# Queries and keys turned by the projection's products and placed by DMAs, in a transformer block written out by hand

## What is computed

```python
x = x + 0.5 * ffn(layernorm(x))      # silu(x @ gate.T) * (x @ up.T), 1024 hidden, @ down.T
x = x + attn(layernorm(x))
x = x + 0.5 * ffn(layernorm(x))
# attn: x_n = x / max(norm(x), 1e-12) * 256 ** 0.5 * gamma
# qkv = x_n @ w_qkv: 16 query heads, 4 key heads, 4 value heads, 64 wide
# q = q * cos + rotate_half(q) * sin; k likewise (cos, sin by row and feature)
# causal softmax(q k.T / 8) v for each head (key head j serves heads j, 4+j, 8+j, 12+j), then @ w_out
```

## Time and profile before

| | us |
|---|---|
| time, median of 3 runs (lowest to highest) | 605.05 (603.68 to 605.48) |
| the profiled execution: its time, and its span | 604.62, 602.8 |
| opening, six turns, ending | 100.0, 416.5, 86.3 |
| busy in the span: PE, DVE, ACT, POOL | 572.0, 494.9, 386.1, 361.9 |
| mean clock granted to PE (1 is 2.4 GHz) | 0.994 |

### The profile page before, as it was taken

One profiled execution on the slowest core, in us unless ns is written; L12 is line 12 of the kernel. 1 busy time (PEld: TensorE's weight loads), 2 busy tenths in 40 slices (PEclk: granted clock), 3 DMA queues, 4 the chain that ended last, 5 costly groups with the idle time before them and its releaser, 6 DMA issues.

```text
span 602.8 us, 13310 instructions
## 1 busy us (share of the span) xinstructions
PE 572.0 (95%) x4230; PEld 531.9 (88%) x4230; DVE 494.9 (82%) x1410; ACT 386.1 (64%) x1021; POOL 361.9 (60%) x322
## 2 busy tenths in 40 slices
PE   6889988999999999999999999999999999878997
PEld 4777777999989999899989999899998999767887
DVE  4879887989789987999879986999879897898642
ACT  4544992499626993489715994379824996279711
POOL 1747764577637673586746775486645766476423
PEclk8989999999999999999999999999999999999999
DMA  7500000000000000000000000000000000000000
GB/s 246 181 15 1 1 2 17 2 2 21 1 17 0 0 17 17 0 0 0 17 17 0 0 17 0 17 0 0 17 17 0 0 0 0 17 2 1 1 18 19
DMA packets 7208, 10.60 MB, mean 18 GB/s; under 512 B 656, under 2 KB 5136, under 8 KB 7184
## 3 DMA queue, kind: packets, MB, share of 16 engines
q1 hardware_dynamic: 7184, 10.29, 5.3%
HBM read 8.19 MB, written 2.10 MB: 17 GB/s over the span
## 4 chain that ended last, share of the span: by engine, by line
PE 66%; DVE 9%; ACT 9%; issue 8%; POOL 6%; DMA 2%; SPq 1%; POOLq 0%; DVEq 0%; ACTq 0%
PE bank L796 46%; PE bank L805 9%; PE bank L883 5%; ACT probs L429 4%; PE bank L861 3%; PE bank L857 2%; DVE xn L579 2%; DVE rope_s L624 2%; POOL hid_lo L313 1%; DMA x_in<-in_x 1%; POOL probs L304 1%; POOL o_t_lo L323 1%; ACT o_sums L441 1%; DVE q_t L600 1%; DVE stats L536 1%
## 5 line engine op out<-in xcount | busy, mean ns | idle before, releaser
L429 ACT ACTIVATE probs<-probs,neg_max 128x128 f32<-128x128 f32 (+1 forms) x256 | 112.9, 448 | 0.2
L304 POOL TENSOR_TENSOR probs<-probs,inv_sum 128x512 f32<-128x512 f32 (+1 forms) x64 | 93.7, 1466 | 31.7 <-DVE inv_sum L660 31.5
L313 POOL TENSOR_TENSOR hid_lo<-hid,hid_hi 128x512 fp32r<-128x512 f32 x64 | 84.1, 1313 | 32.0 <-ACT hid_hi L464 31.8
L796 PE MATMUL bank<-xf_t_hi,gate_hi 128*128 128x256 f32 x256 | 75.0, 293 | 5.9 <-issue 3.1
L796 PE MATMUL bank<-down_hi,hid_hi 128*128 128x256 f32 x256 | 73.6, 288 | 1.0 <-POOL hid_lo L313 1.0
L796 PE MATMUL bank<-xf_t_hi,up_hi 128*128 128x256 f32 x256 | 74.6, 291 | 0.0
L323 POOL TENSOR_TENSOR o_t_lo<-o_sums,o_t_hi 128x512 fp32r<-128x512 f32 x32 | 41.4, 1293 | 53.7 <-ACT o_t_hi L448 53.7
L796 PE MATMUL bank<-down_hi,hid_lo 128*128 128x256 f32 x256 | 72.3, 283 | 0.0
L796 PE MATMUL bank<-down_lo,hid_hi 128*128 128x256 f32 x256 | 72.3, 282 | 0.0
L796 PE MATMUL bank<-xf_t_hi,up_lo 128*128 128x256 f32 x256 | 72.1, 282 | 0.0
L796 PE MATMUL bank<-xf_t_hi,gate_lo 128*128 128x256 f32 x256 | 72.0, 281 | 0.0
(11 more groups left out here) (105 smaller groups left out, 1865.5 us busy)
## 6 DMA issues: line engine op xcount, KB each, us to landing
x_in<-in_x SPq DMA_DIRECT2D x7, 256.0 KB, 2.7
out<-y_out SPq DMA_DIRECT2D x7, 256.0 KB, 2.2
probs<-in_w_qkv SPq DMA_DIRECT2D x4, 384.0 KB, 3.4
probs<-in_w_gate SPq DMA_DIRECT2D x2, 512.0 KB, 6.6
probs<-in_w_up SPq DMA_DIRECT2D x2, 512.0 KB, 6.9
probs<-in_w_down SPq DMA_DIRECT2D x2, 512.0 KB, 4.9
probs<-in_w_out SPq DMA_DIRECT2D x2, 512.0 KB, 5.4
x<-in_x SPq DMA_DIRECT2D x1, 256.0 KB, 2.8
```

The lines of the kernel that those rows point to most:

```text
L304: nc.gpsimd.tensor_tensor(part, part, inv_sum[:, slot].unsqueeze(2).broadcast_to([P, GROUP, keys]), ALU.mult).then_inc(p_done, 1)
L313: nc.gpsimd.tensor_tensor(hid_lo[:, slot].rearrange("p c n -> p (c n)"), hid[:, slot], hid_hi[:, slot].rearrange("p c n -> p (c n)").bitca ...
L429: last = nc.scalar.activation(part, part, ACT.Exp, bias=neg_max[:, slot, g:g + 1], scale=-1.0, accum_out=row_sum[:, slot, g:g + 1])
L796: last = nc.tensor.matmul(dst, a[x], b[y], start=start and i == 0, stop=stop and i == 2, skip_group_check=shared)
```

## The change

In the loop the projection now gives queries and keys already turned: `qk(i)` multiplies 128 columns of the weights by all 256 rows, so that features lie in the partitions. i = 0 are the keys of all heads, i = 1 to 4 the queries of one key head's group. The columns of w_qkv are put in another order on the host, first halves of the heads' features apart from second halves, so that a rotation takes its partner from the neighbouring block of columns. `rope_products(i)` takes two instructions, `rope_add(i)` two, `rope_hi(i)` one on ScalarE (two for the keys), `rope_lo(i)` one, on VectorE for i = 0 and 1 and on GpSimd for the rest. The results lie in `rotated` and `rotated_k`, 32 partitions a head, and DMAs within SBUF place them into `q_t` and `k_t`: 16 for the queries, issued by SyncE, and 8 for the keys, issued by ScalarE, 128 KB each. The values come from a job of their own (`value_rows`, `value_halves`). `q_transposes`, `q_hi`, `q_lo`, `k_hi`, `k_lo` remain in the opening and the ending alone.

The normalised rows are now written by ScalarE as x * scale + shift everywhere; VectorE only computes the shift (`row_shift`). `powers` now also waits until ScalarE has written the rows of the layer before. SyncE's load of the next `x_in` stands behind the store of `y_out`. Three more products on zeros follow the first transposes (`keep_warm(3)`), and the order of the calls is new on all engines.

```diff
-TRANSPOSES = dict(opening=22, turn=21, ending=20)
+TRANSPOSES = dict(opening=22, turn=15, ending=20)
+QK_JOBS = 1 + KV_HEADS
+FIRST = 2
...
+            def q_restack(j):
+                if j == 0:
+                    sp.wait_ge(first_lo, turn.at(first_lo, FIRST * c["K"] + 2))
+                else:
+                    sp.wait_ge(rot_lo, turn.at(rot_lo, (QK_JOBS - FIRST) * c["K"] + j))
+                for g in range(GROUP):
+                    halves = rotation(1 + j)[DH // 2 * g:DH // 2 * g + DH // 2].bitcast(F32)
+                    sp.dma_start(q_t[:, j, g].bitcast(F32), halves.rearrange("p s h n -> p (s h) n")
+                                 ).then_inc(q_in[j], 16)
...
+                q_restack(0), q_restack(1), q_restack(2), q_restack(3), y_store(), x_load()
...
+            def rope_add(i):
+                c_part, s_part = rope_c[:, c["Q"] % 2], rope_s[:, c["Q"] % 2]
+                pool.wait_ge(rope_mul, turn.at(rope_mul, c["Q"] + 1))
+                pool.wait_ge(t_ready, turn.at(t_ready, c["T0"]))
+                to = rotation(i)[:, 1].bitcast(F32)
+                nc.gpsimd.tensor_tensor(to[:, 0], c_part[:, 0], s_part[:, 1], ALU.subtract)
+                nc.gpsimd.tensor_tensor(to[:, 1], c_part[:, 1], s_part[:, 0], ALU.add).then_inc(rope_sum, 1)
...
+            def normal_rows(src, unit=False):
+                act.wait_ge(shift_set, turn.at(shift_set, c["LN"] + 1))
+                rstd = factor if unit else power_out[:, 0]
+                for t in range(NT):
+                    last = nc.scalar.activation(xn[:, t], src[:, t], ACT.Identity, bias=shift[:, t:t + 1],
+                                                scale=rstd[:, t:t + 1])
+            def k_restack(j):
+                act.wait_ge(first_lo, turn.at(first_lo, FIRST * c["K"] + 1))
+                for s in range(2):
+                    halves = rotated_k[DH // 2 * j:DH // 2 * j + DH // 2, s:s + 2].bitcast(F32)
+                    nc.scalar.dma_start(k_t[:, j, s].bitcast(F32), halves.rearrange("p s h n -> p (s h) n")
+                                     ).then_inc(k_in[j], 16)
...
+            def rope_lo(i):
+                dve.wait_ge(rot_hi, turn.at(rot_hi, i + 1))
+                hi, lo = (rotation(i)[:, s].rearrange("p h n -> p (h n)") for s in range(2))
+                nc.vector.tensor_tensor(lo, lo.bitcast(F32), hi.bitcast(F32), ALU.subtract).then_inc(first_lo, 1)
...
+            def qk(i):
+                if i == 0:
+                    pe.wait_ge(t_lo, turn.at(t_lo, c["xa"]))
+                if i < 2:
+                    pe.wait_ge(y_used, turn.at(y_used, c["Y"] - 1 + i))
+                elif i > 2:
+                    pe.wait_ge(rope_mul, turn.at(rope_mul, c["Q"] - 2))
+                first = (HEADS if i == 0 else GROUP * (i - 1)) * DH
+                for h in range(2):
+                    cols = slice(first + h * P, first + h * P + P)
+                    for k in range(KC):
+                        last = product(bank[Q_BANKS[i]][:, h * SEQ:h * SEQ + SEQ], [w[:, k, cols] for w in qkv_w],
+                                       [x[:, k] for x in xa_t], k == 0, k == KC - 1)
...
-            x_transposes("ff")
+            x_transposes("ff"), keep_warm(3)
...
-                qkv(0, 0), qkv(0, 1), qkv(0, 2), qkv(1, 0), x_transposes("ff"), q_transposes("turn", 0, 0)
-                qkv(1, 1), gate(), q_transposes("turn", 0, 2), up(), q_transposes("turn", 0, 1), gate(), qkv(1, 2)
+                qk(0), qk(1), qk(2), qk(3), x_transposes("ff"), qk(4), gate(), value_rows(), up(), gate(), up()
+                scores(0), gate(), scores(1), up(), down(), gate(), scores(0), scores(1), up(), x_transposes("ff")
```

499 lines of the change are left out of this document (293 added, 206 removed).

## The result

The changed kernel took **620.94 us** (median of 4 runs, 616.63 to 623.49) against 605.20 for the kernel before beside it: ratio 1.026, 95% interval 1.022 to 1.029, slower. The profiled execution took 619.64 us with a span of 617.8.

The account below looks back on a forecast made before the run. TensorE bounds the loop. 604.62 us less 5.6 over six turns, plus 2.2 in the opening and 0.3 for its rest and the ending, gives 601.5, on the median 602; range 593.5 to 609.

Parts of the forecast that it names:

- TensorE's work: Loop: dropping six groups of transposes saves 2.7 us a turn; the products' new shape costs nothing.
- The 0.41 us wait goes: Loop: TensorE's 0.41 us wait for VectorE's normalised rows disappears because ScalarE writes them early enough.
- The waits behind VectorE: Loop: new TensorE waits of 0.2, 1.2, 0.8 us, partly because GpSimd's powers run between rope_lo(0) and rope_lo(1); 2.2 a turn.
- lock not paid: Rival, chance 0.20: VectorE's subtractions pass before GpSimd's powers, row_shift meets a gap; turn 67.25 us, kernel 594.5.
- the forecast's 68.5: Loop: forecast turn in us, 66.3 without new waits plus 2.2 of waits, 0.93 less than before.
- The placements: Loop: group 0's queries land 1.7 us after issue, at T+14.4; TensorE wants them at T+16.7, slack 2.3 us.
- DMAs late: Rival, chance 0.15: placements take 6.9 us from issue, TensorE waits 2.9 us a turn, 619 us; decides from 4.8.
- The Trainium skill's rule that I set beside it: 32 partitions reach 8 of 16 ports; at about 218 GB/s queries land at T+17.5, a wait of 1 us a turn.
- ScalarE's issues: Loop: the keys' eight DMA issues cost ScalarE 0.43 us each, 3.4 a turn, fitting its idle time.
- Opening: Rows behind the first weight's split delay the first gate to 14.7; +2.2 us, bounds 0 and +5.
- Ending: Rest of the opening and ending: same work in changed order, +0.3 us, bounds -2 and +2.
- the forecast's own case: The forecast itself, chance 0.42: a time of 599.5 to 605 us.

Follow-up runs that it names:

- run 1: The changed kernel without its 24 placements per turn, scores reading the rows the opening left in q_t and k_t: 600.48 us, ratio 0.992.
- run 2: The changed kernel with all 24 placements issued by SyncE in the order of need, ScalarE issuing none: 599.83 us, ratio 0.992.
- run 3: The changed kernel with all placements on SyncE, all eight of the keys ahead of the queries': 633.74 us, ratio 1.050.
- run 4: Run 2 with the opening's rows first and VectorE's second shift later, but ScalarE issuing the first key head's two placements: 598.04 us, ratio 0.987.
- run 5: The changed kernel with the keys' placements in pieces of 256 bytes instead of 1 KB, same number of issues: 601.36 us, ratio 0.995.
- run 6: The changed kernel with the keys' placements in pieces of 512 bytes instead of 1 KB, same number of issues: 605.10 us, ratio 1.000.
- run 7: The changed kernel with each placement reading one row of 128 partitions instead of four rows of 32, same bytes: 599.35 us, ratio 0.993.
- run 10: The changed kernel with eight unread products on TensorE between the second up and the first scores: 615.17 us, ratio 1.016.
- run 8: The changed kernel with ScalarE's key placements of heads 1 to 3 moved behind its second tanh and rounding: 622.30 us, ratio 1.030.
- the nine profiles: Profiles with the changed kernel's opening order: that kernel and runs 1 to 3, 5 to 8 and 10; loop starts at 100.09 to 104.67 us.

## Why the prediction was wrong, point by point

**TensorE's work** (2.7 us less, the products' new shape free): right. Run 1's turn of 68.2 us less its waits (0.33, 0.84 and 0.75, below) is 66.3, the figure of the forecast. (The busy time of a turn, which counts each product's way through the array, fell by 2.0.)

**The 0.41 us wait goes**: half right. It does, but at the turn's end the transposes of `xn` wait 0.74 us for ScalarE's rows, in all runs in which ScalarE writes them. I had looked only at the rows of the turn's start.

**The waits behind VectorE** (0.2, 1.2 and 0.8 us): the first and last came (0.33 us behind `qk(4)` and 0.84 behind the second `gate`, by the distance from job to job), the second did not. The step that failed is the one with the powers between `rope_lo(0)` and `rope_lo(1)`. VectorE and GpSimd in that turn (timeline):

```profile
398.92 0.69 DVE L747 TENSOR_TENSOR rotated_k<-rotated_k 128x512 fp32r<-128x512 f32 x1
399.52 0.69 DVE L747 TENSOR_TENSOR rotated<-rotated 128x512 fp32r<-128x512 f32 x1
...
399.09 1.39 POOL L315 TENSOR_TENSOR power_out<-power_in,exponent 128x4 f32<-128x4 f32 x1 [1.19 <-DVE less_mean L649]
...
401.92 0.54 DVE L679 TENSOR_TENSOR shift<-less_mean,power_out 128x2 f32<-128x2 f32 x1
```

VectorE's two passed back to back at full speed; GpSimd's powers took 1.39 us for 1.01. `row_shift` lost 0.4, as said. That is the first half of the rival "lock not paid", though not its price: `row_shift` met no gap. That the loop without placements comes near the forecast's 68.5 is luck: a wait of 1.2 us that did not come is made up by one of 0.75 that I had not seen (66.3 + 0.33 + 0.84 + 0.75 = 68.2 us, measured 68.08 to 68.28 in run 1).

**The placements: the step that made the forecast wrong.** "The nearest in size and load is 1.7" and "Slack 2.3 us". The terms as measured: the first group's four issues begin at T+10.2, earlier than the 11.35 forecast (VectorE was not held up), and take 3.72 us, not 1.7, so that the last still starts at T+12.5, as forecast (12.7). It lands 5.3 us later and not 1.7: the scores start at T+17.9, where I had the landing at 14.4. And TensorE is there at T+15.8 (run 2) and not at 16.7, because the 1.2 us wait behind VectorE did not come. The prediction had itself named 4.8 us as the landing from which on the placements decide. The reason (runs 2 to 7): the landing of 1.7 us was that of the last two stores, and I put no transfer in flight beside the one that is waited for. The same view of the kernel before also has two loads of 128 KB among others, which take twice as long and which I passed over (by the forecast's own times even they would have left 0.5 us of slack):

```profile
rope_sb<-in_rope SPq DMA_DIRECT2D x1, 128.0 KB, 3.5
mask_sb<-in_mask SPq DMA_DIRECT2D x1, 128.0 KB, 3.4
```

Between the first issue and the first scores (399.67 to 407.93) the engines moved some 1.5 MB (183 GB/s), where the first scores need 0.79 MB, and once they were full it was 220 GB/s from 32 partitions. The Trainium skill, page DMA: Bandwidth & Descriptors, section Issuing engines are not separate DMA queues, says that transfers run on the same 16 engines and interleave whoever issued them; the changed kernel agrees, where the keys' fifth transfer, issued 0.8 us behind the queries' fourth, landed with it, at T+17.8. The rival "DMAs late" gave 619 us for this. Its way was nearly right: a landing of 6.9 us and a wait of 2.9 where 5.3 and 1.9 to 2.4 were measured. That its 619 lies so near 620.94 is partly luck: its longer wait stands in for the lower clock, which it did not have. The Trainium skill's rule that I set beside it gave 218 GB/s, T+17.5 and a wait of 1 us; measured were 220 GB/s and the first scores at T+17.9.

**What no step had**: the wait costs more than itself. 12.5 us of waits and 5.9 us of lower clock (run 10) make 18.4 of the 19.65 us (429.29 less 409.64) by which the six turns of the changed kernel exceed those of run 2.

**ScalarE's issues** at 0.43 us, "bounds: nothing, and twice as much": the upper bound came (0.90 on the mean). In the changed kernel they held its second tanh until 405.27. VectorE waited 1.65 us for that, but TensorE stood waiting for the placement meanwhile; run 8 shows 4.4 us of issues on the path.

**Opening** (+2.2): +3.25. The mechanism was right (shift and rows behind the first weight), and its size lies within what one opening differs from the next (+0.2 to +4.8 over the nine profiles against the 99.89 of before). The first gate came at 15.37, not at 14.7: `x_lo` ended at 15.0 and not at 13.6, because `x_hi` stood behind a third weight split that ended at 13.8, and the granted clock stayed at 0.50 until 15. The warming products held the gate by 0.4 us more at most. **Ending** (+0.3): -0.74.

With the placements mended and nothing else (run 2) the kernel takes 599.8 us, inside the 599.5 to 605 of the forecast's own case; a loop shorter than forecast (409.64 us for some 411) and an opening of 100.09 have their part in that.

## What to carry to other kernels

Cost a DMA that someone waits for by two sums, not by the landing of one alone: the issues ahead of it on its own queue, and the bytes in flight with it from all queues at the rate for its kind of source; put transfers in the order in which they are needed, across queues too, before thinking about which engine issues them. The order of 24 transfers on one queue was worth 34 us here, where the change with everything mended gains 6 to 8. And a wait of 2 us on TensorE in the middle of a dense loop may cost another 1.5 us in clock: look at the granted clock of the stretch behind it.

## What the runs showed of the hardware

- Transfers of 128 KB within the on-chip buffer in pieces of 1 KB, issued by two engines, with the DMA engines 0.96 to 1.03 busy: 220 GB/s from 32 partitions (the changed kernel, 9 us), 337 GB/s from 128 (run 7, 5 us).
- SyncE alone issues such a transfer every 0.65 us, whatever its place in the order (runs 2 and 3), which is some 200 GB/s with the DMA engines 0.83 to 0.88 busy. With both engines issuing, single ones took 0.55 to 1.69 us in the changed kernel, and SyncE's first four 0.65 us each with a quarter of the keys' bytes (run 5). In run 7 SyncE's first four took 0.46 to 0.62 us each, with the DMA engines 1.02 busy.
- The landing of one such transfer, from its issue: 1.7 us for the last two stores, 2.5 to 2.9 in runs 2, 3 and 7, 5.3 to 5.5 in the changed kernel.
- Idle times of TensorE of the same length (1.93 and 1.94 us) were followed by the lower clock in one turn and not in another; with idle times of 3.5 to 4.0 us (run 3) the turns took 73.4 to 74.7 us.
- Two VectorE instructions with both inputs in the buffer, issued back to back (starts 0.60 us apart, 0.69 each), were not separated by a GpSimd instruction that had come up between them, which took 1.39 us for 1.01, in all six turns.
